# Weighing of values: two heads side by side in one matmul, or one head on each half of the array rows

## The reference, cut to what matters

```python
def local_attention(q, k, v):          # window w = 32, 8 windows; each sees itself and the one before
    bk2, bv2 = (look(bk), look(bv))    # 64 keys and 64 value rows for each window of 32 queries
    sim = jnp.einsum('bhwie,bhwje->bhwij', bq, bk2) * QK_SCALE
    sim = jnp.where(mask, -jnp.finfo(sim.dtype).max, sim)
    attn = jax.nn.softmax(sim, -1)
    out = jnp.einsum('bhwij,bhwje->bhwie', attn, bv2)   # the weighing of values
```

## Time and profile before

| | |
|---|---|
| median of 3 runs | 2605.0 us (2604.25 to 2606.4) |
| profiled execution, its own time | 2607.13 us |
| its span | 2605.3 us |
| PE busy | 2383.1 us, 91% |
| DVE / ACT / POOL busy | 1763.3 / 1625.6 / 1605.3 us |
| the encoder layers | about 190 to 1965 us of the span |

### The profile page before, as it was taken

One profiled execution on the slowest core, in us unless ns is written; L12 is line 12 of the kernel. 1 busy time (PEld: TensorE's weight loads), 2 busy tenths in 40 slices (PEclk: granted clock), 3 DMA queues, 4 the chain that ended last, 5 costly groups with the idle time before them and its releaser, 6 DMA issues.

```text
span 2605.3 us, 57541 instructions
## 1 busy us (share of the span) xinstructions
PE 2383.1 (91%) x22655; PEld 1632.9 (63%) x22655; DVE 1763.3 (68%) x2708; ACT 1625.6 (62%) x3162; POOL 1605.3 (62%) x931
## 2 busy tenths in 40 slices
PE   5769999999999999999999999999997888889998
PEld 3436666666666666666666666666665666656665
DVE  2348777777777777777777777777774888852332
ACT  1127777777777777777777777777773666643332
POOL 1039878887888788878887888788872222301111
PEclk8879999999999999999999999999997999989999
DMA  4002223222232222322233222322223000000000
GB/s 107 0 21 59 53 55 75 69 63 55 59 79 69 55 59 62 78 63 59 53 78 71 59 54 54 87 66 54 54 56 102 1 1 1 1 1 5 5 2 8
DMA packets 77196, 127.11 MB, mean 49 GB/s; under 512 B 24948, under 2 KB 48770, under 8 KB 76930
## 3 DMA queue, kind: packets, MB, share of 16 engines
q1 hardware_dynamic: 76930, 123.42, 20.3%
HBM read 26.56 MB, written 1.07 MB: 11 GB/s over the span
## 4 chain that ended last, share of the span: by engine, by line
PE 45%; DVE 26%; issue 13%; ACT 12%; POOL 4%; DMA 0%; SPq 0%; ACTq 0%; POOLq 0%; DVEq 0%
DVE qk L1211 7%; PE bank L604 7%; PE bank L527 5%; PE bank L563 5%; PE bank L813 4%; PE obank L584 4%; DVE n L1218 4%; PE bank L618 3%; ACT qk L900 3%; DVE bank L1235 3%; PE obank L823 2%; PE bank L823 2%; DVE sh L1227 2%; DVE mx L1223 2%; DVE mx L1365 2%
## 5 line engine op out<-in xcount | busy, mean ns | idle before, releaser
L1211 DVE TENSOR_TENSOR qk<-bank,tab 128x1024 f32<-128x1024 f32 x384 | 468.7, 1221 | 308.4 <-ACT qk L900 308.4
L1519 POOL TENSOR_TENSOR qk<-qk 128x1024 f32<-128x1024 f32 x192 | 454.6, 2368 | 284.0 <-DVE qk L1211 284.0
L1523 POOL TENSOR_TENSOR rn<-n2m,cst 128x16 f32<-128x16 f32 x192 | 562.6, 2930 | 16.0
L527 PE MATMUL bank<-wqk,xs 128*128 128x512 f32 x768 | 404.4, 609 | 46.0 <-ACT kT L926 43.0
L1527 POOL TENSOR_TENSOR qk<-qk,rn 128x1024 f32<-128x1024 f32 x192 | 365.2, 1902 | 28.2 <-POOL rn L1523 0.9
L900 ACT ACTIVATE qk<-bank 128x512 f32<-128x512 f32 x384 | 227.1, 591 | 213.8 <-PE bank L527 208.4
L538 PEld LDWEIGHTS bank<-cst,qk 128*128 128x128 f32 x1536 | 192.3, 141 | 210.5 <-issue 186.4
L1531 POOL TENSOR_TENSOR lnr<-lnv,cst 128x2 f32<-128x2 f32 (+1 forms) x88 | 66.3, 753 | 382.4 <-DVE lnv L1105 382.4
L538 PE MATMUL bank<-cst,qk 128*128 128x128 f32 x1536 | 231.7, 274 | 7.5 <-POOL qk L1527 7.5
L1218 DVE TENSOR_REDUCE n<-qk 128x16 f32<-128x1024 f32 x192 | 232.1, 1209 | 0.0
L912 ACT COPY vp<-lnbank 64x512 f32<-64x512 f32 x384 | 225.0, 586 | 9.4
(11 more groups left out here) (195 smaller groups left out, 4387.8 us busy)
## 6 DMA issues: line engine op xcount, KB each, us to landing
vp<-vp SPq DMA_DIRECT2D x672, 130.0 KB, 2.4
wqk<-in_L_ffn_Wqkv SPq DMA_DIRECT2D x24, 256.0 KB, 3.1
wv<-in_L_ffn_Wqkv SPq DMA_DIRECT2D x6, 512.0 KB, 3.6
wo<-in_L_ffn_Wo SPq DMA_DIRECT2D x6, 512.0 KB, 4.2
xs<-Z SPq DMA_DIRECT2D x48, 64.0 KB, 2.0
xs<-Z SPq DMA_DIRECT2D x48, 63.8 KB, 2.0
kT<-rel_by_distance SPq DMA_DIRECT2D x1, 2048.0 KB, 8.1
vp<-in_L_ffn_w SPq DMA_DIRECT2D x1, 2048.0 KB, 13.2
```

The costliest lines, as they stand in the source:

```text
L527: nc.tensor.matmul(bank[s % 2][:, :], xs[:, odd, WIN + r * P:WIN + r * P + P], wqk[:, lo:lo + 512], start=True, stop=True).then_inc(p_full, 1)
L1211: tt(qk[:, both, :].rearrange("p o (h d) -> p o h d", d=DH), heads(bank[c % 2][:, :]).unsqueeze(1).broadcast_to([P, 2, PAIRS, DH]), table. ...
L1519: tt(direct, direct, swapped, ALU.add).then_inc(sum_done, 1)
L1523: tt(rn[:, m % 2, :], n2m[:, :], const("mhalf"), ALU.pow).then_inc(rn_done, 1)
```

## The change

The weigh of a pair becomes two matmuls. Each takes 64 rows (one head's keys), 65 columns (its values and its ones) and the tile 64*32. The two heads write to two different output banks: `obank[:, 0]` gets first heads, `obank[:, 1]` second heads. `VB` becomes 65, so `vp` has half the size and holds no zeros that matter. ACT copies a value bank in one instruction of 128 partitions, and `v_done` counts once for each. DVE's division reads heads in the new order and writes them in the old one. `mw2` gets memory of its own, as `vp` is now too small for it.

```diff
-VB = 2 * (DH + 1)
+VB = DH + 1
...
-        mw2 = vflat[:, NE * EF:2 * NE * EF].rearrange("p (e c n) -> p e c n", e=NE, c=4)
+        mw2 = sb("mw2", [P, NE, 4, DIM])
...
-                    sp.wait_ge(v_done, 8 * t + 2)
+                    sp.wait_ge(v_done, 4 * t + 1)
...
                     for w in range(4):
-                        mm = nc.tensor.matmul(obank[WIN * w:WIN * w + WIN, q // 2, (q % 2) * VB:(q % 2) * VB + VB],
-                                              pT[:, k % 2, q * P + w * WIN:q * P + w * WIN + WIN],
-                                              vp[:, 4 * r + w, 4 * g + q, :], start=True, stop=True)
+                        for o in range(2):
+                            own = slice(64 * o, 64 * o + 64)
+                            mm = nc.tensor.matmul(obank[WIN * w:WIN * w + WIN, o, q * VB:q * VB + VB],
+                                                  pT[own, k % 2, q * P + w * WIN:q * P + w * WIN + WIN],
+                                                  vp[own, 4 * r + w, 4 * g + q, :], start=True, stop=True)
                 mm.then_inc(o_full, 1)
...
-                for o in (1, 0):
-                    lo = 64 * o
-                    src = vbank[lo:lo + 64, :].rearrange("p (a d) -> p a d", d=DH)
-                    cols = slice(o * (DH + 1), o * (DH + 1) + DH)
-                    nc.scalar.copy(vp[lo:lo + 64, 2 * j + 1, :, cols], src).then_inc(v_done, 1)
+                nc.scalar.copy(vp[:, 2 * j + 1, :, 0:DH], vbank[:, :].rearrange("p (a d) -> p a d", d=DH)).then_inc(v_done, 1)
...
-            nc.vector.memset(vp[0:64, :, :, DH:DH + 1], 1.0)
-            nc.vector.memset(vp[64:P, :, :, VB - 1:VB], 1.0)
+            nc.vector.memset(vp[:, :, :, DH:VB], 1.0)
...
+            def by_pair(ap):
+                return ap.rearrange("p (q o n) -> p o q n", o=2, n=DH)
+
             def divide_out(i, k):
                 b = k % 2
                 dve.wait_ge(o_full, 4 * i + k + 1)
-                o = obank[:, :, 0:2 * VB].rearrange("p c (h n) -> p c h n", n=DH + 1)
-                nc.vector.reciprocal(rd[:, b, :].rearrange("p (c h) -> p c h", c=2), o[:, :, :, DH]).then_inc(rd_done, 1)
+                o = obank[:, :, 0:4 * VB].rearrange("p o (q n) -> p o q n", n=VB)
+                r = rd[:, b, :].rearrange("p (o q) -> p o q", o=2)
+                nc.vector.reciprocal(r, o[:, :, :, DH]).then_inc(rd_done, 1)
                 dve.wait_ge(rd_done, 4 * i + k + 1)
 
                 wait(dve, ot_full, 4 * i + k - 1)
-                tt(ao[:, b, :].rearrange("p (c h n) -> p c h n", c=2, h=4), o[:, :, :, 0:DH],
-                   rd[:, b, :].rearrange("p (c h) -> p c h", c=2).unsqueeze(3).broadcast_to([P, 2, 4, DH]),
+                tt(by_pair(ao[:, b, :]), o[:, :, :, 0:DH], r.unsqueeze(3).broadcast_to([P, 2, 4, DH]),
                    ALU.mult).then_inc(ao_done, 1)
```

More of the change, by code:

```diff
@@ L356, in layer @@
                         load_xs(t + 1, (n + 1) % B, (n + 1) % 2)
-                    sp.wait_ge(v_done, 8 * t + 4)
+                    sp.wait_ge(v_done, 4 * t + 2)
                     spread_values(t, 1, 0)
@@ L369, in layer @@
                         load_w2(l)
-                    sp.wait_ge(v_done, 8 * t + 6)
+                    sp.wait_ge(v_done, 4 * t + 3)
                     spread_values(t, 2, 0)
@@ L378, in layer @@
                         load_o(l)
-                    sp.wait_ge(v_done, 8 * t + 8)
+                    sp.wait_ge(v_done, 4 * t + 4)
                     spread_values(t, 3, 0)
@@ L544, in values @@
                     pe.wait_ge(ld_v, (i // B) * 16 + 16)
-                wait(pe, v_done, 8 * i + 2 * w)
+                wait(pe, v_done, 4 * i + w)
                 for o in range(2):
```

## The result

The change makes the kernel a little slower: 2612.8 us median (2607.5 to 2615.1, 9 runs) against 2605.4 us (2604.3 to 2606.4, 9 runs), ratio 1.0026, 95% interval 1.0016 to 1.0036. The forecast was 2579 us, and "faster". The profiled execution took 2607.49 us (span 2605.5), the fastest of its runs, and almost the 2607.13 us of the one before. So the two traces can be compared at equal time, and something was won that was lost again.

The account below looks back on a forecast made before the run. TensorE (91% busy) was taken as the bound, two of four weighs on the chain. Saving 2 x 0.28 = 0.56 us an item over some 47 items gives 26.3 us: 2579 us from 2605.0, range 2560 to 2621.

Parts of the forecast that it names:

- What bounds the kernel: Per item, weighs of slots 6 and 0 set the time; those of slots 2 and 4 are covered by a 0.91 us wait.
- Step (a): TensorE's weigh: half the columns on twice the tiles, row halves overlapping, 0.43 us less a weigh.
- the mean rate of records is the limit: Slower rival, TensorE's weigh: 64 records at 27 ns, 1.73 us a weigh; +146 us, 2751 us; chance 0.08.
- the load no longer hides: Rival, TensorE's weigh: weight loads show, 0.65 us per tile; 0.07 us less a weigh, -7 us, 2598 us; chance 0.10.
- Step (b): TensorE, from scores to weigh: the new tile shape switch costs 0.15 us a weigh.
- Step (c): Net for TensorE's weigh, column saving minus switch: 0.28 us less each.
- (d): ACT's copies, two of 64x512 becoming one of 128x512: 113 us less ACT work, worth nothing on the path.
- (e): DMA transfers of vp at half the bytes: 0, since nothing on TensorE waits for them.
- (f): DVE's division, blocks of ones, clearing of vp and mw2's own tensor: 0.
- the second rival: Another name for "the mean rate of records is the limit".

Follow-up runs that it names:

- experiments 6 and 7: Kernel before, old blocks and copies, weigh split over row halves only in slots 0 and 6 (6: 2608.2 us) or slots 2 and 4 (7: 2606.1 us).
- experiment 4: Changed kernel with first heads alone, 32 records of 64x65 a weigh, output not the reference's: 2578.5 us, ratio 0.9892 to the kernel before.
- experiment 5: Changed kernel with 130 columns in each matmul over two neighbouring blocks, 32 records a weigh, values not the reference's: 2577.3 us, ratio 0.9893 to the kernel before.
- experiment 3: Changed kernel with the old 16 matmuls of 128x130 over two neighbouring blocks, values not the reference's: 2604.6 us, ratio 0.9992 to the kernel before.

## Why the prediction was wrong

- *What bounds the kernel.* Right in that two weighs of four set the time and two have cover: experiments 6 and 7 give 0.20 us an item and 0.01, 4 and 5 turn 0.28 us a weigh into 27 and 28 us. One thing in it failed, without an effect on the sum: not both covered weighs end in the wait for L926. It grew by slot 4's saving alone (1.01 us in the changed kernel, 1.19 in experiment 5, where 1.5 was forecast for 0.28 a weigh); slot 2's ends at L425, which waits for POOL.
- *Step (a), 0.43 us less a weigh.* This failed. That the halves overlap was right (8 tiles at work within 0.06 us, all columns in 0.60 us in experiment 5). But I weighed the record limit only as a limit on the mean, of 27 ns, read off a burst that streams held to 27 ns anyway. It is neither 27 ns nor absent: 8 ns each for the first 32 records, 12.5 behind them. (a) was taken as 0.43 us and measured 0.24 (1.03 to 0.79). The rival "the mean rate of records is the limit" had the mechanism and a price some six times too high (1.73 us a weigh against the forecast's 0.60, measured 0.79); between it and the forecast I had no middle. The rival "the load no longer hides" came near with 0.07 us net a weigh (measured 0.10), but by another mechanism: it priced a load at 27 ns in each tile's turn, and experiment 4 has 59 ns a turn with its load, where 54 is the stream. In the trace before, 32 records were the whole weigh, so it could not show what follows them; that should have stood as a bound.
- *Step (b), 0.15 us.* Measured 0.14 in slots 0 and 6: 1.01 us from scores to weigh against 0.87 (in slots 2 and 4, 0.11 against 0.90). The Trainium skill (TensorEngine Tiling (Array Packing), "Key Properties") says that a change of tiling mode drains TensorE; the trace agrees, last scores record to first weigh record 0.20 us instead of 0.07, and going from 128 to 64 rows counts as such a change.
- *Step (c), net.* 0.10 instead of 0.28 us, for the weighs of 46 items -9.3 us instead of -26.3 for 47.
- *Steps (d), (e), (f).* Right on the time: experiment 3, no change that can be measured, with ACT's copies at 605 ns where 592 were assumed. ACT's busy time fell by 133 us instead of 113. In all 192 cases the one copy starts 0.11 us before the instruction ahead of it has ended, where the first of the two had started 0.02 us behind it. The single block of ones and the rest did not show.
- *Not in the prediction at all.* What twice as many records in a weigh cost outside its pace: some 13 us of stops in the profiled run, more than the 9.3 us that the weighs won. I counted records as starts in the array, never as a program that has to be brought. The doubled count of the weigh's records was in the diff, and the page of before had a q8 row that I passed over.
- *A rule against the forecast.* The Trainium skill (TensorE: Matmul & The Clock Gate, "Wait — 56ns, not 53.3ns?") says that small matmuls never start closer than about 25 ns. The trace disagrees: 7 ns within a burst over eight tiles, 12.5 ns behind the 32nd record. Worked like the second rival, 64 records at the Trainium skill's figure give an estimate of 0.88 us more a weigh with the switch, 2.6 us an item, some 2730 us in all (the prediction's "about 115" us more is a little low).
- *The range* held the median, for a reason that wasn't in it; the forecast of "faster" at 0.73 did not.

## What to carry to other kernels

Count what a change does to the number of instructions in a dense stretch, and not only to what they compute: here 32 records of 130 columns and 32 of 65 columns were equally well fed, and 64 were not. Halving the array is worth it where the records stay as many (experiment 5: 1.07% faster), so try to give each half more columns; no kernel here does that with the reference's values. When a kernel loses time at "issue" in the middle of a group, compare the instruction queue's packets and the place of the stops in the program before looking for a semaphore, and try moving them with a few instructions that cost nothing. That helped one of the two kernels here fully, the other little.

## What the runs showed of the hardware

- Eight records started 7 ns apart in a weigh over eight tiles, and four within 20 ns (median) in one over four, with the next ones behind a pause. As each matmul leaves two records for one tile, it follows that TensorE ran records for a free tile ahead of those for a busy one; the records don't name their tiles.
- Behind the first 32 records of a weigh (8 ns apart) the other 32, 65 columns over 64 rows and eight tiles, started 12.5 ns apart on the mean.
- TensorE's program comes in packets of 16 KB (3.80 MB in 232), 256 instructions. It stopped for up to 1.9 us at a time, at a count of 193 to 195 modulo 256, and went on 2.2 to 2.8 us after a packet began. An item of 960 instructions had no stops, one of 959 lost 12.7 us in 46 items, with the same work.
- A change from 128*32 to 64*32 tiles cost 0.14 us in slots 0 and 6 and 0.11 in slots 2 and 4.
